# The plan of the attention's side tasks: queries, keys and maxima due one step sooner, and the transposes of the row maxima two steps behind the last maximum

## The reference

```python
q, k, v = jnp.split(xn @ W[idx_s].T + b, 3, axis=-1)           # spatial: no mask
att = softmax(q @ k.T) ; spatial_out = att @ v @ out_w.T
q, k, v = linear(xt)                                           # temporal: causal mask
att = softmax(where(causal, q @ k.T, -inf)); temporal_out = xt + att @ v @ tp_w.T
fused = cross_mha(spatial_out, temporal_out)                   # q of spatial, k and v of temporal: no mask
```

## Time and profile before

| | us |
|---|---|
| median of three runs | 1969.96 |
| lowest of them | 1966.17 |
| the profiled execution, its own time | 1968.53 |
| span of its trace | 1966.7 |
| TensorE busy | 1820.8 (93% of the span) |
| VectorE busy | 1184.8 (60%) |
| ScalarE busy | 723.6 (37%) |

### The profile page before, as it was taken

How to read it: one execution, slowest core, us unless ns; L and a number is a source line. 1 busy time by engine, 2 the same in 40 slices (tenths; PEclk the granted TensorE clock), 3 DMA queues, 4 the chain that set the end, 5 groups by cost and what they waited for, 6 DMA issues and landing times.

```text
span 1966.7 us, 30993 instructions
## 1 busy us (share of the span) xinstructions
PE 1820.8 (93%) x10495; PEld 1624.1 (83%) x10495; DVE 1184.8 (60%) x2343; ACT 723.6 (37%) x1346; POOL 337.7 (17%) x335
## 2 busy tenths in 40 slices
PE   2999999986999999999989999989999999899998
PEld 1788567855899989889889898889999999787996
DVE  7776567775556546663756647656665666675332
ACT  1223211014655435445445554245545444220110
POOL 3210001002212011020100004100000013565440
PEclk9999999988999999999999999999999999999999
DMA  3101001011031000030000000000000001111101
GB/s 108 33 7 44 11 11 32 1 48 44 11 122 38 27 17 6 1 121 12 12 6 11 12 1 12 27 11 12 6 12 6 6 1 62 55 54 48 43 33 52
DMA packets 24783, 58.00 MB, mean 29 GB/s; under 512 B 2538, under 2 KB 4806, under 8 KB 24014
## 3 DMA queue, kind: packets, MB, share of 16 engines
q1 hardware_dynamic: 24650, 56.18, 8.8%
HBM read 44.87 MB, written 11.30 MB: 29 GB/s over the span
## 4 chain that ended last, share of the span: by engine, by line
PE 79%; DVE 12%; issue 3%; DMA 2%; ACT 1%; DVEq 1%; POOL 1%; SPq 0%; POOLq 0%; ACTq 0%
PE ps L2284 19%; PE ps L2169 13%; PE ps L2339 7%; PE ps L1961 6%; PE ps L2266 5%; PE ps L2270 5%; PE ps L2227 5%; PE ps L2368 4%; DVE max_part L1712 4%; PE ps L2055 3%; PE ps L2092 3%; DVE share L1729 2%; PE ps L1974 1%; PE ps L2295 1%; DMA tok_a<-in_x 1%
## 5 line engine op out<-in xcount | busy, mean ns | idle before, releaser
L2284 PE MATMUL ps<-p_raw,v_ones 125*128 125x250 f32 x2080 | 527.0, 375 | 10.5 <-DVE feat L1731 8.4
L1712 DVE TENSOR_REDUCE max_part<-ps 125x2 f32<-125x500 f32 x520 | 330.3, 674 | 236.8 <-PE ps L2227 224.4
L1288 ACT ACTIVATE p_raw<-ps 125x500 f32<-125x500 f32 x520 | 304.3, 586 | 351.3 <-PE ps L2270 346.7
L2284 PEld LDWEIGHTS ps<-p_raw,v_ones 125*128 125x128 f32 x2080 | 360.8, 190 | 37.1 <-issue 9.8
L1729 DVE RECIPROCAL share<-ps 64x250 f32<-64x250 f32 x120 | 206.3, 1719 | 75.5 <-PE ps L2284 72.5
L2266 PE MATMUL ps<-q_both_a,k_both_a 128*125 128x250 f32 x520 | 184.2, 374 | 1.8 <-issue 0.9
L2266 PE MATMUL ps<-q_both_b,k_both_b 128*125 128x250 f32 x520 | 181.8, 371 | 0.0
L1552 DVE TENSOR_SCALAR onehot<-iota_h,win_key,key_t 125x320 f16 x453 | 170.2, 376 | 0.7 <-issue 0.6
L892 POOL CAST w_hi<-w_raw 128x512 fp32r<-128x512 f32 x44 | 28.3, 643 | 825.2 <-issue 359.7
L2169 PE MATMUL ps<-xa_hi,w_hi 128*128 128x418 f32 (+1 forms) x448 | 150.2, 335 | 14.9 <-POOL w_lo L894 9.1
L1551 DVE TENSOR_SCALAR onehot<-iota_h,low_t 125x125 f16 x453 | 126.2, 279 | 59.5 <-PE ps L2092 30.8
(11 more groups left out here) (378 smaller groups left out, 3395.9 us busy)
## 6 DMA issues: line engine op xcount, KB each, us to landing
w_raw<-in_w_mlp SPq DMA_DIRECT2D x32, 256.0 KB, 2.6
w_raw<-in_w_gps SPq DMA_DIRECT2D x16, 256.0 KB, 2.6
w_raw<-in_w_tp SPq DMA_DIRECT2D x16, 256.0 KB, 2.6
w_raw<-in_w_sp SPq DMA_DIRECT2D x12, 256.0 KB, 2.7
w_raw<-in_w_cr SPq DMA_DIRECT2D x12, 256.0 KB, 2.6
d_xt<-xb_hi SPq DMA_DIRECT2D x1, 2508.0 KB, 7.5
d_xt<-xb_lo SPq DMA_DIRECT2D x1, 2508.0 KB, 14.9
xa_hi<-d_xt SPq DMA_DIRECT2D x1, 2508.0 KB, 9.6
```

Of the source, the lines that this page charges most:

```text
L1288: act.activation(p_raw[:, g % PR, :], ps[0:TOK, g % 2, 0:4 * TOK], ACT.Exp, scale=SCALE).then_inc(s_exp, 1)
L1712: dve.tensor_reduce(part[:, y, :, j], ps[0:TOK, bank, 0:4 * TOK].rearrange("p (h k) -> p h k", h=2), AX.X, ALU.max)\
L2284: ins = pe.matmul(ps[:, bank, 0:2 * TOK], v_ones[:, n % 2, kt, h:h + 2, :], p_raw[:, g % PR, cols], start=(b == 0 and x == 0), stop=last)
```

## The change

The due step of every M of a group moves from `gf - 5 - ...` to `gf - 6 - ...`, where `gf` is the group's first step; that of its Q from `gf - 8 - ...` to `gf - 9 - ...`; those of the pass's K follow, since they are counted from the Q of the first group. The due steps of R, V, T and F stay. `allowed` lets an R in two steps behind the last M of its group, in place of one. No instruction is added or taken away; some stand elsewhere in the order, and some tiles in another of the four PSUM banks.

```diff
@@ -177,8 +177,8 @@
             gf, tasks = FIRST[n, i], maxima(n, i)
             due["R", n, i] = gf - 4
             for x, task in enumerate(tasks):
-                due[task] = gf - 5 - 2 * (len(tasks) - 1 - x) // 3
-            due["Q", n, i] = gf - 8 - 2 * len(tasks) // 3
+                due[task] = gf - 6 - 2 * (len(tasks) - 1 - x) // 3
+            due["Q", n, i] = gf - 9 - 2 * len(tasks) // 3
         gf, start = FIRST[n, 0], due["Q", n, 0]
         for p in range(3):
             due["K", n, p] = start - 1 - 4 * (2 - p)
@@ -209,7 +209,7 @@
     if kind == "M":
         return max(later(("Q", n, rest[0]), 1), later(("K", n, 2), 2))
     if kind == "R":
-        return later(maxima(n, rest[0])[-1], 1)
+        return later(maxima(n, rest[0])[-1], 2)
     if kind == "T":
         b = rest[0]
         return max([later(("V", n, 2), 2)] + ([max(uses(n - 2, b)) + 1] if n > 1 else []) + ([later(("T", n, b - 1), 0)] if b else []))
```

## The result

The changed kernel takes 1947.95 us (median of four runs, 1947.55 to 1948.9) against 1969.2 us: the ratio is 0.9901 with a 95% interval of 0.9884 to 0.9918. The 1969.2 us counts in one run of 3506.1 us; the other three have a median of 1968.44.

What follows compares the result with a forecast made beforehand. TensorE was taken as the bound, busy 1820.8 of 1966.7 us. Removed R waits of 3.2 + 3.4 + 1.5 = 8.1 us, off the median 1969.96, gave 1961.9, said as 1962; range 1951 to 1974.

Steps and rivals of the forecast that it cites:

- The bound and the place: Whole kernel: TensorE is the bound, and only its idle time in the four attention stretches, 50.6 us, can be won.
- the openings: At 493.33 and the start of pass 8: R's waits of 3.94 us stay, 7.9 of 19.3 us out of reach.
- The size of a wait: R's waits for `max_col` outside the two fixed lists: priced by idle time shown, 11.4 us in reach.
- 17 waits outside the causal passes: Passes 0 to 2 and 8 to 11: waits of some 0.19 us, all 3.2 us go.
- the end of pass 3: Last part of pass 3: four R waits, the longest 1.17 us, all 3.4 us go.
- both ends that I had named: Whole kernel: 1951 as the range's low end; 1949.6 with all 11.4 us and 9 us from order won.
- The causal passes: Passes 4 to 7: of 4.9 us of R's waits, 2.4 are paid elsewhere and 1.5 us are won.
- the moves of the other tasks: Maxima, queries and keys a step sooner: order-dependent waits change by -9 to +9 us, taken as 0.
- Rival (a): Whole kernel: nothing is won, since TensorE arrives earlier at waits VectorE sets; 1967 to 1973 us, chance 0.22.
- (b): Causal pass starts: reductions brought ahead of `unit_out` delay products by 20.5 us; 1984 us, chance 0.06.
- (c): Maxima behind their query: half of 9.9 us of waits also goes; 1957, down to 1950 us, chance 0.15.
- (d): Four low-clock stretches: removed waits lift the granted clock, 10.4 us more, 1951.5 us, chance 0.02.

## Why the prediction was wrong

*The bound and the place* were right: all of the gain lies in the attention, on TensorE's waits, and the openings stayed at 3.9 us each.

*The size of a wait* was the first term off: outside the causal passes 6.6 us were forecast and 11.3 measured. I took the idle time of the rows, 3.2 us for 17 waits outside the causal passes and 3.4 us at the end of pass 3. Matmuls are pipelined, and a record is longer than the distance to the next one. Before the change, ahead of the R at 574.53:

```profile
573.96 0.28 PE L2266 MATMUL ps<-q_both_b,k_both_b 128*125 128x250 f32 x1
574.08 0.28 PE L2270 MATMUL ps<-q_row_b,k_rest_b 128*125 128x250 f32 x1
```

Two such matmuls start 0.12 us apart. R starts 0.45 us behind the last, so TensorE lost 0.33 us, where the row shows 0.18. In the same way the 1.17 us at 842.68 stand for 1.44 - 0.12 = 1.32. With 0.15 us more for each of the 29 waits, the 11.4 us in reach are 15.8. For the four passes 8 to 11 this makes 11 x 0.34 = 3.7 us in place of 2.1, of 5.3 us measured. A wait for a bank (0.5 us) and 0.3 us of the products' waits for `p_raw` go there too; the last 0.8 I do not trace to single waits. R alone moved gave 4.8 us there and 5.7 us in passes 0 to 3, where the idle times promised 2.1 and 4.5, so the correction points the right way by experiment too. The Trainium skill, Perfetto Trace Analysis, section "Tensor Engine Instruction (MATMUL, LD_WEIGHTS)", says that the end of a matmul in a profile is an estimate from the instruction's size and no measurement; the rows agree, with 0.28 us of record on 0.12 us of distance.

The time lies below both ends that I had named, 1951 and 1949.6.

*The causal passes* were the step that failed: 1.5 us forecast for passes 4 to 7, 8.9 measured in 4 to 6. Two terms of the sum did it. R's removed waits were to come back at the products, so that the waits for `feat` rise by 2.4 us to 10.8; they fell to 6.2. And the moves of the other tasks were taken as 0 ("-9 to +9 us, and take 0"); the waits of maxima behind a query fell by 3.9 us. "Without R's wait TensorE only comes earlier to the product and waits 0.81 us more there" is right as a mechanism: the start of pass 7 shows it, 2.53 us for 1.34, and with R moved by hand the idle time of passes 4 to 6 does not fall (19.1 us for 17.8). Wrong was to follow R alone and take the rest of the plan as fixed. A step holds three tasks; R's leaving opened a place, and the planner put a key layer of 2.3 us into TensorE's wait. Taking this layer back costs 3 to 6.5 us and adding it to R's move wins 5.9. The sign could have been had by working out which task comes next where R leaves a full step.

*Rival (a)*, that waits only move, holds in the causal passes for R moved alone; *(b)*, reductions in front of `unit_out`, did not come true, but its mirror image did: `unit_out` in front of the reductions won 8 us. *(c)*, more by order, was the right rival with too small a price and for another reason: the waits behind a query fell by only 3.9 us (7.6 + 2.3 to 6.0), and 1.3 us behind a key came in.

*(d)*, the clock, I had set aside too surely. With R alone moved the granted clock fell in the causal passes, where it had been 1.00 before. Its windows of 40 us (columns as in rows 2):

```profile
900.00:940.00 40.00, 36.26 (x236) 33.80 (x235) 21.66 (x33) 18.80 (x38) 1.88 (x2) 0.95 0.03 7
1100.00:1140.00 40.00, 35.27 (x213) 33.39 (x214) 32.19 (x46) 17.76 (x34) 1.90 (x2) 0.96 0.02 8
1180.00:1220.00 40.00, 36.40 (x230) 33.91 (x229) 33.16 (x45) 15.37 (x32) 12.45 (x16) 0.91 0.00 1
```

From 940 to 980 us it is 0.96 as well. If TensorE bound all of it, that is up to 40 x (0.05 + 0.04 + 0.04 + 0.09) = 8.8 us, an upper end, since part of the time VectorE did; the longer busy time of passes 4 to 6 alone is 4.5 us. Over all runs the mean granted clock is 0.9738 with R alone and 0.9774 before, which by the same estimate is 7 us at most. So the larger part of what R alone loses in passes 4 to 6 is clock and not waits; how much of its whole time is stays open between these estimates.

What the engine did before the clock fell can be counted. In all ten kernels whose openings keep R's wait of 3.94 us, the clock is lowered right behind it, in both openings (0.50, the level of 1.2 GHz, from 493 to 499 us and from 1292 to 1297 in the kernel before). In the three that fill this wait it is 1.00 there (from 488 to 512 us with the openings changed). Ten bare waits of 2.5 us for `unit_out` stand in six of the kernels, the changed one among them; the clock fell within 1.5 us of the end of eight of them. Of the eight starts of pass 5 or 6 in which a key layer fills this wait, none has a fall. So a removed or filled wait can be worth more than its length, as rival (d) has it. The gain in passes 4 to 6 itself holds none of this: the clock is 1.00 there before and after.

The Trainium skill, TensorE: Matmul & The Clock Gate, section "A second HAM failure mode: psum-queue depth-cycling", lets micro-idles between matmul groups bring the clock down. I wrote that the trace disagrees; with R alone it agrees, at 0.91 to 0.96, and the openings of the kernel before agreed already. But 35.43 us busy in 40 kept 1.00 before, so the busy share alone does not tell when.

## What to carry to other kernels

Price a stall on a pipelined engine by the distance from start to start, less the usual one, and not by the gap that a row shows: small gaps were worth nearly twice their face. In a planned order, a task that moves leaves a place; ask what fills it, and whether the bottleneck's next wait then has work in it or not. Where a wait cannot be removed because another engine's unbroken row sets it, put work into it or change what stands first in that row: here this was worth 3 to 6.5 and 8 us. Before a difference of a few us is put down to waits, compare busy time and granted clock of the same instructions: with R alone, 4.5 of 5.8 us were longer busy time.

## What the runs showed of the hardware

The granted clock can fall and rise again within the causal passes, by order alone, with the same instructions: from 900 to 1220 us four stretches of 40 us are under 1.00 with R alone, one in the changed kernel (0.96 from 1140), none before. It was lowered behind all twenty waits of 3.94 us and behind eight of ten bare waits of 2.5 us, and behind none of the eight that a key layer filled. The times follow it: the run of R alone with 0.977 takes 1959.46 us, the ten with 0.972 to 0.974 take 1962.42 to 1966.0. The 21 runs of the kernel before beside them lie between 1964.83 and 1970.2 us.
